# A graph network with four attention blocks: vector products on GpSimd, table loads placed by hand, and a perceptron taken one tile at a time

## The reference, cut to what matters

```python
x = x + relational_layer_5(...)            # what the five layers give
h = relu(layernorm(x))
h = relu(gat_conv(h, W1, a_src1, a_dst1, b1, heads=4))   # first attention, 4 heads of 64
h = gat_conv(h, W2, a_src2, a_dst2, b2, heads=1)         # second attention, 256 wide
x = x + relu(relu(h) @ Wm1 + bm1) @ Wm2 + bm2            # the perceptron
h = relu(layernorm(x))
h = elu(gat_layer(h, ..., heads=8)); x = x + gat_layer(h, ..., heads=1)

def gat_conv(x, src, dst, W, a_src, a_dst, bias, heads):
    h = (x @ W).reshape(n, heads, -1)
    alpha_s = (h * a_src[None]).sum(-1)
    alpha_d = (h * a_dst[None]).sum(-1)
    e = leaky_relu(alpha_s[src] + alpha_d[dst], 0.2)
    m = segment_max(e, dst)
    e = exp(e - m[dst])
    alpha = e / (segment_sum(e, dst)[dst] + 1e-16)
    return segment_sum(h[src] * alpha[:, :, None], dst).reshape(n, -1) + bias
```

## Time and profile before

| | us |
|---|---|
| median of 3 runs | 839.83 |
| lowest and highest | 837.68, 840.53 |
| the profiled execution | 841.04 |
| its span | 839.2 |
| TensorE busy | 788.2 (94%) |
| VectorE busy | 604.9 (72%) |
| ScalarE busy | 411.9 (49%) |
| GpSimd busy | 484.8 (58%) |

### The profile page before, as it was taken

The page is one execution under the profiler, slowest core; times in us unless marked ns, Lnnn a source line. Parts: engine busy times, 40 slices in busy tenths (PEclk is TensorE's granted clock), DMA queues, the critical chain, the costliest instruction groups (busy, mean ns, idle before and its releaser), DMA issues.

```text
span 839.2 us, 10361 instructions
## 1 busy us (share of the span) xinstructions
PE 788.2 (94%) x4112; PEld 637.7 (76%) x4112; DVE 604.9 (72%) x665; ACT 411.9 (49%) x487; POOL 484.8 (58%) x211
## 2 busy tenths in 40 slices
PE   7999999999879999988988899999999999888998
PEld 4669976786546799667656569999999999765674
DVE  8965249999998622989899988555986496554442
ACT  6514366676763442776766724444444433142411
POOL 0626519999996471799989936731971486000000
PEclk9999999999999999999999999999999999989999
DMA  9037516344431553450444238545455453700001
GB/s 366 21 95 243 167 49 170 89 137 138 144 112 47 194 174 113 111 140 1 150 139 129 97 114 300 190 150 188 151 191 189 145 202 120 281 3 1 0 1 39
DMA packets 24409, 111.01 MB, mean 132 GB/s; under 512 B 3620, under 2 KB 6180, under 8 KB 23976
## 3 DMA queue, kind: packets, MB, share of 16 engines
q1 hardware_dynamic: 23240, 104.24, 38.3%
q10 hardware_dynamic: 1120, 6.10, 1.8%
HBM read 100.63 MB, written 0.79 MB: 121 GB/s over the span
## 4 chain that ended last, share of the span: by engine, by line
PE 63%; DVE 19%; POOL 13%; ACT 3%; issue 1%; DMA 0%; DVEq 0%; ACTq 0%
PE ps L991 28%; DVE prod L1832 10%; POOL prod L556 10%; PE ps L957 7%; PE ps L1022 5%; PE ps L1468 3%; DVE qi_t L1850 3%; POOL prod L559 3%; PE ps L1328 2%; PE ps L1149 2%; PE ps L1170 2%; PE ps L1281 2%; PE ps L1527 2%; PE ps L1453 1%; PE ps L1150 1%
## 5 line engine op out<-in xcount | busy, mean ns | idle before, releaser
L544 POOL TENSOR_TENSOR w_lo<-w_raw,w_hi 128x1536 fp32r<-128x1536 f32 x49 | 183.5, 3756 | 142.6 <-ACT w_hi L621 142.5
L556 POOL TENSOR_TENSOR prod<-prod 128x1024 f32<-128x1024 f32 x94 | 222.8, 2390 | 47.1 <-DVE prod L1832 46.9
L755 ACT ACTIVATE prod<-ps 128x1024 f32<-128x1024 f32 x192 | 187.4, 1023 | 74.2 <-PE ps L1281 62.3
L1832 DVE TENSOR_TENSOR prod<-prod,ps 128x2048 f32<-128x2048 f32 x96 | 217.7, 2279 | 8.4 <-ACT prod L755 5.2
L621 ACT ACTIVATE w_hi<-w_raw 128x1536 fp32r<-128x1536 f32 x60 | 88.9, 1487 | 119.3 <-PE ps L991 108.8
L1281 PE MATMUL ps<-sel_pair,h_and_q 128*128 128x512 f32 x384 | 129.6, 450 | 16.3 <-ACT prod L755 16.0
L991 PE MATMUL ps<-w_hi,yt_hi 128*128 128x384 f32 x480 | 122.9, 336 | 0.0
L991 PE MATMUL ps<-w_hi,yt_lo 128*128 128x384 f32 x480 | 121.8, 334 | 0.0
L991 PE MATMUL ps<-w_lo,yt_hi 128*128 128x384 f32 x480 | 121.8, 334 | 0.0
L1281 PEld LDWEIGHTS ps<-sel_pair,h_and_q 128*128 128x128 f32 x384 | 67.7, 192 | 51.6 <-ACT prod L755 30.9
L957 PE MATMUL ps<-w_raw,h_t 128*128 128x384 f32 x312 | 106.8, 486 | 0.0
(11 more groups left out here) (212 smaller groups left out, 1049.3 us busy)
## 6 DMA issues: line engine op xcount, KB each, us to landing
w_raw<-weights SPq DMA_DIRECT2D x105, 768.0 KB, 4.4
wa_in<-weights SPq DMA_DIRECT2D x6, 768.0 KB, 5.9
w_gat<-weights SPq DMA_DIRECT2D x6, 768.0 KB, 8.2
w_query<-weights SPq DMA_DIRECT2D x3, 768.0 KB, 11.8
h_and_q<-stage_hi SPq DMA_DIRECT2D x24, 96.0 KB, 2.1
h_and_q<-stage_lo SPq DMA_DIRECT2D x24, 96.0 KB, 2.2
a_vec<-gat_vectors ACTq DMA_DIRECT2D x1, 2048.0 KB, 9.5
q_t<-queries ACTq DMA_DIRECT2D x1, 1536.0 KB, 12.1
```

Source lines behind the costliest of these rows:

```text
L544: pool.tensor_tensor(Wl[:, j, :], raw_slab(U, 0, j), Wh[:, j, :], ALU.subtract).then_inc(w_lo_by_pool, 1)
L556: pool.tensor_tensor(v[:, :, 0:32], v[:, :, 0:32], v[:, :, 32:64], ALU.add).then_inc(folded_once, 1)
L755: act.activation(slot_view(s)[:, :, 32 * u:32 * u + 32], args.rearrange("p b (n l) -> p (b n) l", l=LH), ACT.Sigmoid).then_inc(sigmoid_rea ...
L1832: TT(slot_view(s), slot_view(s), ps[:, 6, o:o + L].unsqueeze(1).broadcast_to([P, NB, L]), ALU.mult).then_inc(products_ready, 1)
```

## The change

Six edits. GpSimd makes the two vector products of the first attention, after its last low half, into `wa_tmp` and `wa_in`; VectorE only sums them (`first_weights`), the first sum after the residual of tile 0. A small sigmoid and a small exponential are issued ahead, so that the table loads stand there. In the first attention ScalarE copies the logit rows of tile 1 before h. The vector products of the second attention are issued on VectorE before the low half of the logit rows of tile 1, where they were after the maxima. The second block of the first attention is turned by products with the identity. The perceptron's first layer is made tile by tile, in banks 6 and 5.

```diff
--- before.py
+++ after.py
@@ -321,6 +321,7 @@
         wa_in_read = sem("wa_in_used")
         wa_zero = sem("wa_zero")
         wa_product = sem("wa_product")
+        wa_product_by_pool = sem("wa_product_by_pool")
         wa_ready = sem("wa_ready")
         w31_landed = sem("w31_landed")
         w32_landed = sem("w32_landed")
@@ -610,6 +611,13 @@
             for layer in range(2, LAYERS):
                 for v in range(RELATIONS[layer]):
                     w_lo(UNIT[layer] + 1 + v)
+            wait_landed(pool, 30, 0, 0)
+            pool.wait_ge(wa_ready, 2)
+            hn, c, o_s, o_d, _ = GAT[0]
+            for tmp, o in ((wa_tmp, o_s), (wa_in, o_d)):
+                pool.tensor_tensor(tmp[:].rearrange("p (k f) -> p k f", k=KC), raw_slab(30, 0, 0).rearrange("p (k f) -> p k f", k=KC),
+                                   av[:, o:o + hn * c].unsqueeze(1).broadcast_to([P, KC, hn * c]),
+                                   ALU.mult).then_inc(wa_product_by_pool, 1)
             for n in (2, 3):
                 for t in range(NT):
                     rstd(n, t)
@@ -727,6 +735,8 @@
 
             for i in range(2):
                 relations(i)
+                if i == 0:
+                    act.activation(small[:, 120:121], mhalf[:, 0:1], ACT.Sigmoid)
 
                 acc = pair(i, 0)
                 U = UNIT[i] + 4
@@ -838,6 +848,7 @@
                 act.wait_ge(qi_ready, STEPS * (i + 1))
                 w_hi(UNIT[i + 1] + 1, (0,))
 
+            act.activation(small[:, 121:122], mhalf[:, 0:1], ACT.Exp)
             act.wait_ge(query_copied, 2 * STEPS // 8)
             act.wait_ge(products_ready, 2 * STEPS)
             act.dma_start(gb[:], gbias.partition_broadcast(P)).then_inc(vectors_in, 16)
@@ -895,8 +906,8 @@
             first_half(0, 4, 6, False)
             relu_norm(2, 1, norm_h_ready)
             rows_hi(0, 0)
+            rows_hi(0, 1)
             keep_h(0, 0)
-            rows_hi(0, 1)
             leaky(0, 0)
             leaky(0, 1)
             exponential(0, 0)
@@ -910,10 +921,11 @@
             exponential(1, 0)
             keep_h(1, 1)
             first_half(2, 3, 2, True)
-            act.wait_ge(mlp_done, 1)
-            for k in range(2):
-                act.activation(MT[:, k, :], ps[:, 6, k * N:(k + 1) * N], ACT.Relu,
-                               bias=small[:, 30 + k:31 + k]).then_inc(mt_ready, 1)
+            for t in range(NT):
+                act.wait_ge(mlp_done, t + 1)
+                for k in range(2):
+                    act.activation(MT[:, k, t * P:(t + 1) * P], ps[:, 6 - t, k * P:(k + 1) * P], ACT.Relu,
+                                   bias=small[:, 30 + k:31 + k]).then_inc(mt_ready, 1)
             act.wait_ge(norm_ready, 7)
             for h in range(2):
                 act.activation(H[:, 0, h * FH:(h + 1) * FH], X[:, 0, h * FH:(h + 1) * FH], ACT.Relu, scale=small[:, 48:49],
@@ -1506,9 +1518,11 @@
                     pe.wait_ge(g_exp_ready, EBASE[g] + sum(len(q) for q in BLOCKS[g][:u]) + n + 1)
                     for s in range(NT):
                         o = u * 1024 + n * N + s * P
-                        ins = pe.transpose(turned_piece(g, u).rearrange("p b n -> p (b n)")[:, (s * len(p) + n) * P:
-                                                                                           (s * len(p) + n + 1) * P],
-                                           zb[:, o:o + P], ident[:])
+                        piece = turned_piece(g, u).rearrange("p b n -> p (b n)")[:, (s * len(p) + n) * P:(s * len(p) + n + 1) * P]
+                        if g == 0 and u == 1:
+                            ins = pe.matmul(piece, zb[:, o:o + P], ident[:], start=True, stop=True)
+                        else:
+                            ins = pe.transpose(piece, zb[:, o:o + P], ident[:])
                 ins.then_inc(g_exp_turned, 1)
 
             def weight(g, t, h, d):
@@ -1569,17 +1583,18 @@
 
             for t in range(NT):
                 transpose_tile(t, gout, gout_ready, 2, 2, (3, 7)[t])
-            pe.wait_ge(ht0_ready, 3)
-            pe.wait_ge(ht1_ready, 3)
-            for c in range(2):
-                for k in range(2):
-                    o = 2 * N + k * N + c * P
-                    ins = pe.matmul(ps[:, 6, c * N:(c + 1) * N], W30[:, o:o + P], HT[:, k, :], start=(k == 0), stop=(k == 1))
-            ins.then_inc(mlp_done, 1)
+            for t in range(NT):
+                pe.wait_ge((ht0_ready, ht1_ready)[t], 3)
+                for c in range(2):
+                    for k in range(2):
+                        o = 2 * N + k * N + c * P
+                        ins = pe.matmul(ps[:, 6 - t, c * P:(c + 1) * P], W30[:, o:o + P], HT[:, k, t * P:(t + 1) * P],
+                                        start=(k == 0), stop=(k == 1))
+                ins.then_inc(mlp_done, 1)
             for t in range(NT):
                 for h in range(2):
                     for k in range(2):
-                        pe.wait_ge(mt_ready, k + 1)
+                        pe.wait_ge(mt_ready, 2 * t + k + 1)
                         o = 4 * N + k * F + h * FH
                         ins = pe.matmul(ps[:, 2 * t + h, 0:FH], MT[:, k, t * P:(t + 1) * P], W30[:, o:o + FH],
                                         start=(k == 0), stop=(k == 1))
@@ -2005,11 +2020,18 @@
                 dve.wait_ge(residual_added, t + 1)
                 norm_stats(2, t)
 
-            wait_landed(dve, 30, 0, 0)
-            logit_weights(0, raw_slab(30, 0, 0), 0, 6, False, (0,))
+            def first_weights(side, tmp):
+
+                hn = GAT[0][0]
+                dve.wait_ge(wa_product_by_pool, side + 1)
+                ch.step(dve.tensor_reduce(Wa[:, WB[0]:WB[0] + KC, 32 * side:32 * side + hn],
+                                          tmp[:].rearrange("p (k h c) -> p k h c", k=KC, h=hn), AX.X, ALU.add))
+
             last_residual(0)
+            first_weights(0, wa_tmp)
             norm_shift(2, 0)
-            logit_weights(0, raw_slab(30, 0, 0), 0, 6, True, (1,))
+            first_weights(1, wa_in)
+            dve.nop().then_inc(wa_ready, 1)
             last_residual(1)
             norm_shift(2, 1)
 
@@ -2104,11 +2126,11 @@
             ones_column(0)
             rows_lo(0, 0)
             second_half(0, 6, 6, False)
+            wait_landed(dve, 30, 0, 1)
+            logit_weights(1, raw_slab(30, 0, 1)[:, 0:2 * N], 0, 2, True)
             rows_lo(0, 1)
             for u in range(2):
                 negated_max(0, u)
-            wait_landed(dve, 30, 0, 1)
-            logit_weights(1, raw_slab(30, 0, 1)[:, 0:2 * N], 0, 2, True)
             for u in range(2):
                 counted(0, u)
             for d in range(NT):
```

## The result

The changed kernel takes 831.11 us (median of 5 runs, 829.25 to 831.37). The kernel before, run beside it, takes 838.43 (5 runs, 836.46 to 840.53). The ratio of their means is 0.9905 with a 95% interval of 0.9882 to 0.9928, so 8.0 us faster, between 6.0 and 9.9; the medians differ by 7.3. The profiled execution took 829.25 (span 827.4), against 841.04 for the profiled one before.

The account below looks back on a forecast made before the run. TensorE, or gates binding it to GpSimd and VectorE, bound it to 708 us, then waits between engines. Terms -0.6 -0.7 -2.0 -3.1 -1.1 = -7.5 from 841.04 gave 833.5; median forecast 832.8, range 830.5 to 837.0.

Parts of the forecast that it names:

- Vector products by GpSimd: Hand-over to the attention blocks: two products of 3.5 us on GpSimd bring the second residual sooner, gain 0.7 us.
- The order on the shared port: Hand-over: VectorE's last low half goes first, ending at 712.33; GpSimd's products then run 712.3 to 715.8 and to 719.4.
- The rival of late products: Hand-over: slow GpSimd products delay the root and VectorE; kernel slower, 5.5 us at 10 us a product; chance 0.05.
- the one of a first call: Hand-over: GpSimd's first product pays 6 us once, turning the term from -0.7 to +5.3, so 838.8; chance 0.02.
- Rows copied first, table, order: First attention: logits 0.55 us sooner, exponentials without a table load before them, weighted sums 2.0 us sooner in all.
- The clock: First attention: full clock holds through the weighted sums (1.9 us) and the pieces behind (1.2), gain 3.1 us.
- The second low stretch (757.3 to 760.6): Late half-clock stretch behind a pause, taken to stay, no gain counted; 1.1 us if it went too.
- the 0.7 taken off for the median: Whole kernel: the sum gave 833.5 for the profiled execution; 832.8 was forecast for the median of runs.
- the fall came on the pause and the transposes ahead of them: First attention: claimed cause of the half clock in the weighted sums; without that pause the clock stays full.
- Perceptron: First layer tile by tile: tile 0 starts when the second transposes end, outputs at 763.1, gain 1.1 us.
- Sigmoid's table: Start of the gates: the first sigmoid gains 0.7 us without its load; 0.6 us carried on through the gates.

Follow-up runs that it names:

- transposes only: Changed kernel with the first attention's second block turned by transposes again: 830.23 us, ratio 0.9904 to the kernel before; 109.55 from the transposes after the layers to the end.
- products alone: Kernel before with one edit, the first attention's second block turned by products with the identity: 836.25 us, ratio 0.9971 to the kernel before.
- a pause of 1.36: Changed kernel with the second attention's vector products back behind the maxima on VectorE, second block still turned by products: 833.90 us, ratio 0.9936 to the kernel before.
- the vector products on VectorE again: Changed kernel with the first attention's vector products on VectorE in the old order, none on GpSimd: 832.42 us, ratio 0.9924 to the kernel before.

## Why the prediction was right or wrong

The sign was right, and so was the mechanism of each part but the clock's. 832.8 was forecast and 831.11 measured as the median; the low end of 830.5 was too high for single executions: the profiled one took 829.25. The step that failed is the sum from one execution: it gave the low stretches of the clock that the change does not aim at (one left as it was, three in the gates not noticed) no term, and in the two profiles they are 4.0 of the 11.8 us.

*Vector products by GpSimd* (-0.7): right, 0.8 to 0.9. The order on the shared port was not mine: GpSimd began its product while VectorE made its low half and waited inside it (5.03), with the same end. The rival of late products did not occur; nor did the one of a first call (no product took over 5.03). One ground against the late products was thinner than it reads: of pow on GpSimd the rows have one column only (0.56, rows 1), which shows no rate.

*Rows copied first, table, order* (-2.0): right, 0.61 to the logits (0.55) and 1.53 to the weighted sums (1.45). The idle before the logits is 0.46 (I had asked for 0.4 or less). The four VectorE instructions now bind the logits: without them in the way they come 0.7 to 0.8 sooner.

*The clock* (-3.1): this is the term that was mis-sized, and in two places. The term took the weighted sums at 1.9 and the pieces behind them at 1.2; they gave 1.76 and 0.76. But "The second low stretch (757.3 to 760.6) ... I leave it" left 1.1 out: that stretch is absent from both profiles of the changed kernel and from seven of the ten others that share its order or most of it. And there was no term for the low stretches inside the gates. They come and go from one execution to the next. The execution from which I summed had three, costing about 2.9 us; the profiled one after had none. So -7.5 from 841.04 stood on an execution near the slow end of its kernel (835.4 to 841.5 in 43 executions), and the 0.7 taken off for the median was not enough. The sum that fits: 8.0 from the transposes on, of which 1.1 is the second low stretch and again partly luck, 0.6 for the sigmoid, 2.9 by luck, 0.3 for the start of the gates (116.42 and 116.11), together 11.8, the distance of the two profiled executions. Against medians, 7.0 us were forecast (839.83 to 832.8), 7.3 came and the ratio gives 8.0, so the forecast of the median is near in part by luck: two terms at nothing met a base near the slow end. 1.4 of the 1.7 by which 832.8 is too high is that the median of the kernel before itself came out at 838.43 beside it.

The cause that I gave for the clock ("the fall came on the pause and the transposes ahead of them") was half right: either the pause taken away (transposes only, 109.55) or the transposes replaced (products alone) will do in these traces, but with a pause of 1.36 the replacement did not, and the replacement alone had itself cut the pause from 1.04 to 0.63. Sixteen transposes with no pause behind them let the clock fall in none of the four profiles that have them (for one, 3.06 us of turning, then weighted sums of 3.78).

*Perceptron* (-1.1): right in kind, 1.5 in size: from the start of the second transposes to the outputs it takes 2.06 (750.32 to 752.38), and I had 2.52 (760.58 to 763.1), since tile 0 starts before these transposes have ended and two times four matmuls take 1.79, not 1.95. *Sigmoid's table* (-0.6): right, 0.58.

What stays open is what decides, from one execution to the next, whether the second low stretch and those in the gates come: products, pauses and order were varied, and neither appeared or vanished with any of them. What they have in common can be read from the traces, and is told in the last section: each stands right behind waits of TensorE.

## What to carry to other kernels

Before a table of gains is summed from one profile, look for low stretches of the granted clock where the change does nothing, and for the waits of TensorE ahead of them, price them by the executions' spread, and take the sum against the median, since both profiles may be lucky or unlucky in them. When TensorE turns something and then waits, it is worth finding which engine's queue makes it wait: here moving four VectorE instructions into an earlier hole took away a wait of 1.4 us and the half clock behind it, 3.2 us together. Real products for transposes, which also fill part of the wait, are a second remedy, worth having only where the wait can't go (2.4 us alone, -0.4 on top of the other).

## What the runs showed of the hardware

**Run-to-run spread goes with the clock.** Over 43 executions of the kernel before, the mean granted clock went from 0.988 to 0.996 and the time from 841.0 (mean of the six at 0.988) down to 836.0 (of the eight at 0.996), with a correlation of -0.88. A stretch of 3.4 us at half clock is 0.002 of the mean, and the slope is 1.3 us for each. None of the 43 was above 0.996, which is what the 6.8 us at the weighted sums alone would leave; the changed kernel reached 1.000 in 2 of 11, both times at 829.25 us.

**Every low stretch stands behind waits of TensorE.** The fourteen profiles have 27 falls of the clock, 19 of them in the gates, and these stand at a few places only: 251 to 252 us (five profiles), 375 to 377 (four), 392 (two), 402 and 433 (the kernel before) and 448 to 449 (six). In the 3.4 us ahead of each of the 27, as long as a low stretch itself, TensorE was busy for 1.2 to 2.4 us. For the fall at 252.2 in the kernel before, TensorE in order of time, and the window ahead of the fall:

```profile
250.85 2.50 PE L1328 MATMUL ps<-prod,ident 128*128 128x128 f32 x16 [2.15 <-POOL prod L556]
```

```profile
248.80:252.20 3.40, 1.35 (x12) 1.38 (x13) 3.40 (x3) 1.74 (x2) 3.40 (x2) 1.00 0.35 145
```

The changed kernel's first profile has the same wait at the same place, and no fall behind it:

```profile
250.07 2.02 PE L1340 MATMUL ps<-prod,ident 128*128 128x128 f32 x16 [2.14 <-POOL prod L557]
```

```profile
246.60:250.00 3.40, 1.33 (x5) 0.49 (x3) 3.40 (x3) 2.12 (x3) 3.40 (x3) 1.00 0.63 219
```

So such waits were ahead of every fall but did not always bring one; the second low stretch is alike (the waits of 1.29 and 0.88 ahead of it stand in the profiles with it and without it). What decides between the executions no run here shows. A stretch doesn't cost the same everywhere either: from the first gate arguments to the transposes, a profile with the one near 449 alone takes 601.24 (the vector products on VectorE again), no more than the 601.39 with none, and one with that near 376 alone takes 602.56.

**GpSimd and VectorE take turns by whole instructions.** With all vector products on GpSimd, its product of 128x512 (two in 2.53 us) fell on VectorE's one-column shift, and that took 1.17 instead of 0.16:

```profile
716.91 2.53 POOL L625 TENSOR_TENSOR wa_tmp<-w_raw,a_vec 128x512 f32<-128x512 f32 x2
```

```profile
717.05 1.17 DVE L1703 SCALAR_TENSOR_TENSOR small<-small 128x1 f32<-128x1 f32 x1 [0.44 <-POOL small L551]
```

The shift ends at 718.22, when half of GpSimd's 2.53 are over (718.18). The Trainium skill ("SBUF — State Buffer", Who interferes with whom) has an instruction of either engine hold the shared port whole while the other blocks; the trace agrees (1.17 beside GpSimd, 0.16 alone). This is the loss at the hand-over: the shift releases ScalarE's normalization of tile 0, whose h TensorE turns first, so the transposes start 0.78 later, and the second residual, 1.0 later against the last products of the layers (1.82 after the start of their last two records, 0.82 in the changed kernel). A GpSimd multiply with a repeated operand costs 3.51 for 128x1536, the same as its subtraction, with no dearer first call.
